# Four order edits in a four-layer kernel: fillers of the first norm, the last gate, the query banks, the first pair's queries

## The reference, cut to what matters

```python
x = x + _L0_attn_ref(_layernorm(x), ...)   # state-space layer, 128 heads of 64
x = x + _L0_ffn_ref(_layernorm(x), ...)    # 1792 hidden units, one of each 32 is kept
x = x + _L1_attn_ref(_layernorm(x), ...)   # latent attention, 32 heads
x = x + _L1_ffn_ref(_layernorm(x), ...)    # dense layer masked by clusters
```

```python
idx = jnp.argmax(blk, axis=-1) + jnp.arange(0, INTER, SPARSITY)
h = jax.nn.relu(jnp.einsum('bkm,bm->bk', w1[idx], xf))
out = jnp.einsum('bk,bkm->bm', h, w2t[idx])
```

```python
scores = jnp.einsum('bhqd,bhkd->bhqk', q, k) / np.sqrt(Q_HEAD)
o = jnp.einsum('bhqk,bhkv->bhqv', softmax(scores), v)
```

## Time and profile before

| | |
|---|---|
| median of 3 runs | 2125.84 us |
| the profiled execution: its time, its span | 2125.86 us, 2124.1 us |
| PE busy | 2070.6 us (97%) |
| DVE, ACT, POOL busy | 1596.8, 1455.8, 783.1 us |
| clock granted to PE, mean | 0.995 |

### The profile page before, as it was taken

The page is one execution under the profiler, slowest core; times in us unless marked ns, Lnnn a source line. Parts: engine busy times, 40 slices in busy tenths (PEclk is TensorE's granted clock), DMA queues, the critical chain, the costliest instruction groups (busy, mean ns, idle before and its releaser), DMA issues. The chain is left out here.

```text
span 2124.1 us, 34964 instructions
## 1 busy us (share of the span) xinstructions
PE 2070.6 (97%) x13464; PEld 1689.6 (80%) x13468; DVE 1596.8 (75%) x1762; ACT 1455.8 (69%) x3148; POOL 783.1 (37%) x428
## 2 busy tenths in 40 slices
PE   8899999999999999999999999999799989999998
PEld 7788888888888888888888888887587758888876
DVE  6778788877877878887887787788623347878776
ACT  4777776777677778677777777773633358787872
POOL 2244444544354445444435444544344300101011
PEclk9999999999999999999999999999999999999999
DMA  3222222222132213222222221222042110101001
GB/s 106 110 90 72 98 104 76 80 100 80 70 109 81 96 74 110 71 79 100 80 88 91 93 86 70 104 85 52 30 135 90 51 44 21 31 21 31 13 3 40
DMA packets 56244, 157.51 MB, mean 74 GB/s; under 512 B 16656, under 2 KB 27152, under 8 KB 47632
## 3 DMA queue, kind: packets, MB, share of 16 engines
q1 hardware_dynamic: 56080, 155.28, 21.3%
HBM read 152.64 MB, written 2.62 MB: 73 GB/s over the span
## 5 line engine op out<-in xcount | busy, mean ns | idle before, releaser
L630 PE MATMUL PS<-xnh,wh 128*128 128x512 f32 x1272 | 509.5, 401 | 3.0 <-DVE arena L1699 1.8
L632 PE MATMUL PS<-xnh,wl 128*128 128x512 f32 x1272 | 497.3, 391 | 0.0
L631 PE MATMUL PS<-xnl,wh 128*128 128x512 f32 x1272 | 496.2, 390 | 0.0
L1693 DVE SCALAR_TENSOR_TENSOR arena<-PS,arena 128x1020 f32<-128x1020 f32 (+2 forms) x240 | 305.6, 1274 | 31.1 <-ACT arena L1270 25.4
L1231 ACT ACTIVATE PS<-x,arena 128x128 f32<-128x128 f32 x1024 | 307.8, 354 | 21.0 <-DVE arena L1725 20.0
L630 PEld LDWEIGHTS PS<-xnh,wh 128*128 128x128 f32 x1272 | 239.3, 188 | 57.6 <-issue 8.2
L451 POOL TENSOR_TENSOR zl<-arena,zh 128x1024 fp32r<-128x1024 f32 x63 | 176.8, 2807 | 293.7 <-ACT zh L1253 293.7
L632 PEld LDWEIGHTS PS<-xnh,wl 128*128 128x128 f32 x1272 | 239.1, 188 | 51.7
L631 PEld LDWEIGHTS PS<-xnl,wh 128*128 128x128 f32 x1272 | 239.6, 188 | 46.1
L447 POOL TENSOR_TENSOR arena<-arena 128x1024 f32<-128x1024 f32 x63 | 151.9, 2411 | 297.9 <-ACT arena L1249 297.9
L436 POOL TENSOR_TENSOR wl<-arena,wh 128x1024 fp32r<-128x1024 f32 x72 | 174.8, 2428 | 198.6 <-ACT wh L1220 198.6
(11 more groups left out here) (266 smaller groups left out, 4192.7 us busy)
## 6 DMA issues: line engine op xcount, KB each, us to landing
x<-decay SPq DMA_DIRECT2D x64, 1024.0 KB, 4.6
arena<-in_w_xg SPq DMA_DIRECT2D x72, 512.0 KB, 5.5
arena<-in_w_o SPq DMA_DIRECT2D x32, 512.0 KB, 3.5
arena<-in_w_f SPq DMA_DIRECT2D x28, 512.0 KB, 3.5
x<-in_x SPq DMA_DIRECT2D x3, 1024.0 KB, 6.8
arena<-in_w_h SPq DMA_DIRECT2D x16, 192.0 KB, 2.9
arena<-in_w_h SPq DMA_DIRECT2D x16, 129.0 KB, 2.8
out<-x SPq DMA_DIRECT2D x8, 256.0 KB, 2.1
```

The lines of the kernel that those rows point to most:

```text
L630: mm(PS[:, bank], ah, bh, start=(n == 0), stop=False)
L631: mm(PS[:, bank], ah, bl, start=False, stop=False)
L632: last = mm(PS[:, bank], al, bh, start=False, stop=(n == len(terms) - 1))
L1693: ins = stt(o, pair_of(bank).rearrange("p q (b t) -> p q b t", t=SEQ)[:, :, :, :SEQ - k], w[:, 3 - k:4 - k], o, ALU.mult, ALU.add)
```

## The change

The diff has four parts. (1) The fillers of the first norm: 24 become 40, 16 become 22, 12 and 12 become 14 and none. (2) `split` and `weigh_in` take a function `pause` that is called ahead of the last term; `hidden(1)` gets `first_part(15)` that way, ACT rounds the first gate ahead of the last piece of the mask, and DVE's sum into `x` after block 13 stands behind the gate of block 14. (3) Queries (0, 3) and (1, 1) get banks `Y0` and `Y1`, and wait for no query. (4) `latent_A(1)` stands ahead of `scores(0)`, and queries (0, 2) and (0, 3) stand ahead of the first two turns, on PE, ACT and DVE.

```diff
         def query_bank(i, j):
-            return C if i == 0 and j == 1 else A
+            return {(0, 1): C, (0, 3): Y0, (1, 1): Y1}.get((i, j), A)
...
-                busy(16, S)
+                busy(22, S)
...
-                for h in range(2):
-                    spread(n, h)
-                    busy(12, C + h)
+                spread(n, 0)
+                busy(14, C)
+                spread(n, 1)
...
-            def split(bank, terms):
+            def split(bank, terms, pause=None):
                 for n, (ah, al, bh, bl) in enumerate(terms):
+                    if pause and n == len(terms) - 1:
+                        pause()
...
-            busy(24, A)
+            busy(40, A)
             layernorm(0, ([("x_in0", 16)], [("x_in1", 16)]), sd=sd)
...
-            hidden(1)
-            first_part(2 * NU - 1)
+            hidden(1, lambda: first_part(2 * NU - 1))
...
-                if i or j > 1:
+                if i == 0 and j == 2:
+                    pe.wait_ge(s["ql"], 1)
+                elif i == 1 and j == 0:
+                    pe.wait_ge(s["ql"], 3)
+                elif query_bank(i, j) == A and j + i:
                     pe.wait_ge(s["ql"], 4 * i + j)
...
+            pe.wait_ge(s["ln_xn"], 6)
+            latent_A(1, Y0)
             for w in range(0, NV + 6, 2):
...
-                if w == 0:
-                    pe.wait_ge(s["ln_xn"], 6)
-                    latent_A(1, Y0)
...
+                if w == 2:
+                    query(0, 2)
+                    query(0, 3)
                 for u in (w, w + 1):
                     if 2 <= u < NV + 2:
                         turn_p(u - 2)
                 for u in (w, w + 1):
-                    if u in QUERY_AT:
+                    if u in QUERY_AT and w > 2:
...
+            gate_high(0)
+            mask_part(2 * NU - 1)
...
-                if 2 <= w < NV + 2:
+                if 2 < w < NV + 2:
                     copy(w - 2)
                 if w < NV:
                     exp(w + 1)
+                if w == 2:
+                    query(0, 2)
+                    query(0, 3)
+                    copy(0)
...
+            for n in range(NF):
+                gate(n)
+                if n == FT1:
+                    second_sum(0)
...
-                if w - 1 in QUERY_AT:
+                if w == 3:
+                    query(0, 2)
+                    query(0, 3)
+                elif w - 1 in QUERY_AT and w > 4:
                     query(*QUERY_AT[w - 1])
```

More of the change, by code:

```diff
@@ L633, in split, with weigh_in @@
                 return last
-            def weigh_in(bank, k, part, h):
+            def weigh_in(bank, k, part, h, pause=None):
                 return split(bank, [(wh[:, k, col(part * KD + kk)], wl[:, k, col(part * KD + kk)],
-                                     xnh[:, kk, half(h)], xnl[:, kk, half(h)]) for kk in range(KD)])
+                                     xnh[:, kk, half(h)], xnl[:, kk, half(h)]) for kk in range(KD)], pause)
             pe.wait_ge(s["cst_in"], 16)
             pe.wait_ge(s["dt_set"], 1)
-            busy(24, A)
+            busy(40, A)
             layernorm(0, ([("x_in0", 16)], [("x_in1", 16)]), sd=sd)
@@ L880, in first_part, with hidden @@
                 last.then_inc(s["first_ps"], 1)
-            def hidden(n):
+            def hidden(n, pause=None):
                 pe.wait_ge(s["fw1l"], n + 1)
@@ L885, in hidden @@
                     pe.wait_ge(s["hs"], n - 1)
-                weigh_in(A + n % 2, n % 2, 0, n // FT1).then_inc(s["h_ps"], 1)
+                weigh_in(A + n % 2, n % 2, 0, n // FT1, pause).then_inc(s["h_ps"], 1)
             def down(n):
@@ L1082, in _ @@
                     scores(w)
-                if w == 0:
-                    pe.wait_ge(s["ln_xn"], 6)
-                    latent_A(1, Y0)
-                if w < NV:
                     scores(w + 1)
@@ L1434, in _, with gate_high @@
                     rounded(v // 2 - 5, 1, "f_out")
+            def gate_high(n):
+                ac.wait_ge(s["hs"], n + 1)
+                if n >= 2:
+                    ac.wait_ge(s["f_out"], n - 1)
+                act(zh[:, n % 2, 0:HALF], hs[:, n % 2], ACT.Copy).then_inc(s["hs_h"], 1)
+            gate_high(0)
             mask_part(2 * NU - 1)
@@ L1439, in _ @@
                     rounded(n + 1, 0, "h_ps")
[L1440 to L1443, removed]
+                if n:
+                    gate_high(n)
                 if 1 <= n < NF - 1:
@@ L1892, in _, with gate @@
                    ALU.is_equal).then_inc(s["eq"], 1)
-            for n in range(NF):
+            def gate(n):
                 k, h = n % 2, n // FT1
@@ L1901, in _, with second_sum @@
                 tt(zl[:, k, 0:HALF], hs[:, k], zh[:, k, 0:HALF].bitcast(F32), ALU.subtract).then_inc(s["hs_l"], 1)
-                if n % FT1 == FT1 - 1:
-                    ve.wait_ge(s["f_out"], n + 1)
-                    tt(x[:, :, half(h)], x[:, :, half(h)], PS[:, C:C + KD], ALU.add).then_inc(s["x2"], 1)
+            def second_sum(h):
+                ve.wait_ge(s["f_out"], FT1 * h + FT1)
+                tt(x[:, :, half(h)], x[:, :, half(h)], PS[:, C:C + KD], ALU.add).then_inc(s["x2"], 1)
+            for n in range(NF):
+                gate(n)
+                if n == FT1:
+                    second_sum(0)
                 if n == FT1 + 4:
@@ L1912, in _ @@
                     tt(in_pairs(xn[:, :, half(0)]), in_pairs(xn[:, :, half(0)]), paired_row(), ALU.mult).then_inc(s["ln_xn"], 1)
+            second_sum(1)
             ve.wait_ge(s["x2"], 2)
```

## The result

The changed kernel took 2108.49 us (median of 4 runs, 2107.02 to 2110.63), the kernel before beside it 2126.14 us (4 runs, 2125.33 to 2127.19): 17.65 us less, a ratio of 0.9917 with a 95% interval of 0.9900 to 0.9935. The forecast was 2110.4 us, range 2108.0 to 2114.3: the result lies in the range, 0.5 us above its lower end.

The account below looks back on a forecast made before the run. PE, busy 2070.6 of 2124.1 us, was taken as the bound, so each removed wait gains. Terms 0.4 + 2.0 + 1.9 + 11.2 = 15.5 us off 2125.86 gave 2110.4 us, range 2108.0 to 2114.3.

Parts of the forecast that it names:

- Part 1: First norm: longer steady fillers let the clock rise earlier, so DVE's subtractions start sooner; gain 0.4 us.
- The bounds of -0.6 and +0.65: First norm: limits in us on the fillers' gain, depending on whether the clock rises in time.
- Part 2a: End of the mask: `down(0)` starts at 1527.55 in place of 1529.58; gain 2.0 us.
- part 2b: Between the second layer's halves: block 14's gate is made before DVE's sum, ending PE's wait; gain 1.9 us.
- The wait expected at the mask's end: Ahead of `down(0)`: a wait of some 0.5 us replaces the wait for the gate's rest.
- Parts 3 and 4: Attention's start: new banks and order remove waits and slow stretches up to query (1, 2); gain 11.2 us.
- The walk: Attention's start: new order timed with old durations, query (1, 2) starting at 1733.4 in place of 1744.74.
- those at the turns and ahead of query (1, 2): Attention's start: new waits of 0.3 us in the turns and 0.25 us ahead of query (1, 2).
- The prediction's three stretches: Stretches of 3.3 to 3.4 us at 1.2 GHz behind PE waits, two in attention's start; each costs 1.7 us.
- The eviction chain: Attention steps 2 to 7: if ACT and DVE pace them, L991's 4.3 us of waits only move; 2114.7 us, 9%.
- DVE is no bound: Attention's 64 slots: rival that DVE sets the pace, losing above 4.89 us a slot; 2132.8 us at 5.0, 2%.
- One slow stretch more goes: First state-space tile: the stretch at 67.10 comes without a clock fall, 1.7 us less; 2108.7 us, 12%.

Follow-up runs that it names:

- e1: Kernel before with only the first norm's new filler counts: 2124.69 us, ratio 0.9999.
- e12: Changed kernel with the first norm's old fillers, on a chip that also ran the changed kernel: 2107.82 us, ratio 0.9919.
- e9: The changed kernel, unaltered, timed a second time beside the kernel before: 2107.51 us, ratio 0.9917.
- e11: Changed kernel, latent's rest on DVE in step 1, queries (0, 2), (0, 3) rounded ahead of `exp(3)`, rests ahead of `norm(2)`: 2107.33 us.
- e8: Changed kernel with DVE making the latent's rest for query (0, 2) in step 1 in place of step 2: 2106.86 us, ratio 0.9911.
- e4: Kernel before with only part 4, the new order of `latent_A(1)` and queries (0, 2), (0, 3), and old banks: 2118.37 us, ratio 0.9967.
- e5: Changed kernel with the first norm's old fillers (24, 16, 12, 12): 2107.18 us, ratio 0.9915.
- e7: Kernel before with only `latent_A(1)` moved ahead of the first scores, on PE and ACT: 2122.36 us, ratio 0.9988.
- e2: Kernel before with only part 2, the mask's end, gate rounding and DVE's sum into `x`: 2121.24 us, ratio 0.9982.
- e6: Kernel before with fillers put into two of PE's waits at attention's start, order unchanged: 2123.92 us, ratio 0.9990.
- e10: Kernel before with part 3's banks, and DVE making the rest of query (0, 3) in step 3 in place of 4: 2117.20 us, ratio 0.9958.
- e3: Kernel before with only part 3, own banks for queries (0, 3) and (1, 1): 2121.63 us, ratio 0.9986.

## Why the prediction was right, and where it was short

**What bounds the kernel.** Right. PE was the bound, and each wait that went was a gain.

**Part 1, the fillers, +0.4 us.** Not confirmed and too small to be refuted: e1 is 0.7 us off with an interval that holds zero, and e12 is 0.3 above e9. What the profiles don't bear out is the ground for choosing +0.4, that "4.2 us of steady fillers in one piece is more than what came before the rise". With 40 fillers the first statistics ran wholly at the higher level in 3 of 5 profiles (e1, e9, e11; not in the changed kernel's own and e8), with 24 in 4 of 9 (e4, e5, e7, e12). The bounds of -0.6 and +0.65 were too narrow for one execution as well, since they left out the input's landing. The Trainium skill, "TensorE: Matmul & The Clock Gate", "What's actually happening", has it that the monitor's windows run freely and not anew with a kernel, so that the point of the rise varies. The traces agree with the second half: with 24 fillers the statistics ran at the higher level from 7.03 us on in e5, and at the lower one from 8.03 on in the earlier trace rows.

**Part 2a, 2.0 us; part 2b, 1.9 us.** Right: 1.99 and 1.83 in the trace, 4.2 us for both in e2. The wait expected at the mask's end, some 0.5 us, is 0.31. The sum gives these waits no price in clock. In the earlier trace rows none was paid. But in 4 of the 7 profiles with the old order of the gate (e1, e4, e6, e10) a slow stretch stands right behind the wait of 2.34 us, in none of the 7 with the new order. At 1.7 us each that is about 1.0 us on average, an estimate. The stretches of e1 (busy times as above, PEclk third from the end), whose `down(0)` begins at 1525.31 behind that wait:

```profile
1525.00:1528.00 3.00, 2.69 (x7) 2.20 (x8) 1.45 (x3) 0.63 (x1) 1.28 (x1) 0.61 0.00 0
1528.00:1531.00 3.00, 3.00 (x12) 2.38 (x12) 0.00 (x0) 1.03 (x2) 0.32 (x1) 0.82 0.00 0
```

**Parts 3 and 4, 11.2 us.** The walk held almost step by step. From the end of query (0, 1), at 1698.51 + 0.39, to query (1, 2) 30.0 us were forecast and 29.7 measured; the wait ahead of query (0, 2) is 1.12 (forecast 1.0), that of the scores 0.32 (0.65), those at the turns and ahead of query (1, 2) didn't come. `latent_A(1)` alone, 3.55 in the walk, measured 3.7 by medians and 2.6 by its ratio, and its profile shows only the wait gone.

**The sum, 15.5 us, measured 17.65.** The waits were sized right; the mis-sized term is the clock. The prediction took it from the two slow stretches in attention's start of the earlier trace rows, 3.4 us in all, and from one profile. Two other executions of the same order of attention, e1 and e2, over the same stretch:

```profile
1698.12:1744.65 46.53, 37.48 (x175) 25.11 (x171) 20.11 (x39) 21.75 (x55) 0.00 (x0) 0.85 0.13 39
```

```profile
1695.12:1741.88 46.76, 37.73 (x175) 25.06 (x171) 20.11 (x39) 21.74 (x55) 0.00 (x0) 0.85 0.14 38
```

The idle time is that of before (9.05 and 9.03 against 9.43), but the products take 37.5 and 37.7 us in place of 34.49. The four profiles that have the whole attention part (the changed kernel, e5, e9, e12) agree within 0.02 us: 32.29 to 32.31, all at PEclk 1.00. So the same change is worth 11.6 us against the one profile and 14.2 to 14.5 against the two others. These two are executions with much slow time: their mean granted clock was 0.993, as in 5 of 57 executions of the kernel before.

How large the clock's part is on average can be estimated, since the mean granted clock of each execution was taken too, to 0.001. It is 0.9948 over the 57 executions of the kernel before, and 0.9976 over the 16 of the changed kernel, e5, e9 and e12. That makes 22 us at the lower level against 10. What takes 12 us there takes 6 at the higher one, so the clock gave about 6 us, not 3.4. With the waits that went, 8.0 us in attention and 3.8 in part 2, the sum is 17.8; the means lie 17.5 us apart. The same sum for each run, with the waits from its one profile and the clock from all its executions beside the kernel before on its chip:

| run | waits that went | clock, estimate | both | measured, by means |
|---|---|---|---|---|
| e1, fillers | 0 | 0.2 | 0.2 | 0.1 |
| e2, gate | 3.8 | 0.8 | 4.6 | 3.8 |
| e3, banks | 3.2 | 0.0 | 3.2 | 2.9 |
| e4, order | 3.4 | 5.0 | 8.4 | 7.1 |
| e6, waits filled | 0 | 2.3 | 2.3 | 1.9 |
| e7, latent first | 2.3 | 0.2 | 2.5 | 3.0 |
| e10, banks and rest | 5.7 | 3.8 | 9.5 | 9.0 |
| e9, changed kernel | 11.8 | 5.8 | 17.6 | 17.5 |

So e3 and e7 took waits away and gained no clock, e6 gained clock and took no wait away, and the whole change did both. Where the further 2.6 us of clock lie is shown in part only: in attention by the two profiles above, and behind the gate's wait. The prediction's three stretches are not all of that trace's (PEclk is 0.50 from about 26, 1494 and 1511 us as well), and such stretches outside of attention come and go between executions of either kernel.

The result is inside the range by 0.5 us only, and the room for it came from a rival whose place, the first state-space tile, the profiles don't bear out. That much is luck.

**Given back later.** From query (1, 2) to the end the changed kernel takes 379.96 us and the profile shown of before 379.36. That looked like 0.6 us lost, but e1 and e2, with the old order, take 379.75 and 379.72. About 0.2 us is left: the first slot of two steps takes 4.87 us in place of 4.65.

**The rivals.** None of those that cost came. The eviction chain did move a wait of 1.12 us, not 4.3. DVE is no bound: the slots after it are as before. "One slow stretch more goes", at 2108.7 us, comes nearest to the time, but its place, the first state-space tile, isn't shown: in the changed kernel's own profile that stretch only came later, near 82 us; in those of e8, e11 and e12 there is none, but in those of e1 and e10, without the change, there is none either.

## What to carry to other kernels

A chain of small waits of PE can cost more than their sum, because here the granted clock fell behind many of them and the products after them ran at half speed. Taking them all away at attention's start gave 8 us of waiting and, against three profiles, 3.6 to 6.9 us of clock; taking away one (e7) or filling two (e6) gave its own part and left the falls behind the others. Size the clock's part from several executions of the kernel before: the waits repeat to 0.4 us, the slow stretches don't, and the mean granted clock of many executions tells more than the stretches of one profile. And a buffer of its own for a result does little for a consumer whose operand is made by an engine that stands, in its own order, behind work that needs that same consumer (e3 against e10): check the order of every engine before counting on a bank.

## What the runs showed of the hardware

- Three executions with the same order at the start of attention, and idle times there within 0.4 us, needed 34.49, 37.48 and 37.73 us for the same 175 rows of products, by the granted clock alone (0.92, 0.85, 0.85).
- In six profiles of the start of attention with no wait of PE over 1.12 us, PEclk never left 1.00 there. In e10, waits of 1.94 and 1.14 us had no slow stretch behind them either, while in e3 the same first wait of 1.93 us had one: behind a wait of this size a fall came in some executions and not in others.
- The landing of the input's second half varied between 9.30 and 11.88 us over the profiles, with unchanged DMA code. With the clock's rise it makes the first norm differ by some 3 us between executions.
